# Idle transposes ahead of the first product, and two gate products of the third node tile re-ordered, in a graph network and expert kernel

## The reference

```python
h = layernorm(x)
m = relu(concat(h[src], edge_attr) @ W1.T + b1) @ W2.T + b2
agg = segment_sum(m, dst)
gi, gh = agg @ W_ih.T + b_ih, h @ W_hh.T + b_hh        # three thirds each: r, z, n
r, z = sigmoid(i_r + h_r), sigmoid(i_z + h_z)
n = tanh(i_n + r * h_n)
x1 = x + h + batchnorm((1 - z) * n + z * h)
```

```python
h2 = layernorm(x1)
f1 = h2 @ [Wg | W1 | Ws1]      # 8 gate logits, 256 expert units, 32 shared units
comb = softmax of the two largest gate logits, at their experts
out = x1 + (relu(expert units) * comb) @ W2 + shared part
```

## Time and profile before

| | |
|---|---|
| Median of 3 runs | 1315.35 us (1314.4 to 1319.97) |
| The profiled execution's own time | 1303.76 us |
| Its span, first to last instruction | 1301.9 us |
| Mean granted TensorE clock | 0.999 |
| Busy: TensorE, GpSimd, VectorE, ScalarE | 1281.2, 816.4, 997.7, 734.0 us |

### The profile page before, as it was taken

One profiled execution on the slowest core, in us unless ns is written; L12 is line 12 of the kernel. 1 busy time (PEld: TensorE's weight loads), 2 busy tenths in 40 slices (PEclk: granted clock), 3 DMA queues, 4 the chain that ended last, 5 costly groups with the idle time before them and its releaser, 6 DMA issues. The chain is left out here.

```text
span 1301.9 us, 22928 instructions
## 1 busy us (share of the span) xinstructions
PE 1281.2 (98%) x6398; PEld 1083.2 (83%) x6398; DVE 997.7 (77%) x2198; ACT 734.0 (56%) x1726; POOL 816.4 (63%) x1117
## 2 busy tenths in 40 slices
PE   8999999999899999999999999999999999999997
PEld 7788888888688888888888888888888888888885
DVE  6879575568777777777777777777777777777776
ACT  5331222134666666666666666666666666666652
POOL 3121243114777777777777777777778777777771
PEclk9999999999999999999999999999999999999999
DMA  8123554377433433333433433433433433433430
GB/s 297 43 83 135 198 198 162 125 273 240 141 132 130 135 122 129 137 121 129 137 121 129 136 121 129 136 122 129 137 121 129 137 121 129 137 121 129 136 98 33
DMA packets 64208, 179.58 MB, mean 138 GB/s; under 512 B 9456, under 2 KB 10352, under 8 KB 64048
## 3 DMA queue, kind: packets, MB, share of 16 engines
q1 hardware_dynamic: 48160, 99.20, 22.3%
q0 software_dynamic: 16016, 79.97, 18.6%
HBM read 141.86 MB, written 37.29 MB: 138 GB/s over the span
## 5 line engine op out<-in xcount | busy, mean ns | idle before, releaser
L1844 PE MATMUL bank<-whh_hi,x_hi 128*128 128x512 f32 x948 | 376.7, 397 | 2.4 <-DVE x L1774 1.6
L1844 PE MATMUL bank<-whh_hi,x_lo 128*128 128x512 f32 x948 | 370.1, 390 | 0.0
L1844 PE MATMUL bank<-whh_lo,x_hi 128*128 128x512 f32 x948 | 369.7, 390 | 0.0
L1844 PEld LDWEIGHTS bank<-whh_hi,x_hi 128*128 128x128 f32 x948 | 178.2, 188 | 38.6 <-DVE x L1774 2.0
L1844 PEld LDWEIGHTS bank<-whh_hi,x_lo 128*128 128x128 f32 x948 | 178.0, 188 | 37.8
L1844 PEld LDWEIGHTS bank<-whh_lo,x_hi 128*128 128x128 f32 x948 | 178.3, 188 | 34.3
L1593 POOL TENSOR_TENSOR h_n<-h,n_gate 128x512 f32<-128x512 f32 x78 | 101.0, 1294 | 68.7 <-ACT n_gate L1612 68.7
L1525 POOL TENSOR_TENSOR rstd<-var_eps,minus_half 128x1 f32<-128x1 f32 x158 | 90.4, 572 | 66.0 <-DVE var_eps L505 65.9
L1733 DVE TENSOR_TENSOR h_lo<-bank,h_hi 128x512 fp32r<-128x512 f32 x79 | 54.7, 692 | 77.8 <-ACT h_hi L1660 77.8
L1510 POOL DMA_INDIRECT gates<-gates_in,slot_at x78 | 83.7, 1074 | 46.7 <-issue 45.7
L1587 POOL TENSOR_TENSOR n_pre<-r_hn,gates 128x512 f32<-128x512 f32 x77 | 99.2, 1288 | 13.0 <-POOL r_hn L1583 13.0
(11 more groups left out here) (214 smaller groups left out, 3101.9 us busy)
## 6 DMA issues: line engine op xcount, KB each, us to landing
xt<-in_x SPq DMA_DIRECT2D x79, 256.0 KB, 2.8
x_lo_raw<-in_x_cols SPq DMA_DIRECT2D x79, 256.0 KB, 2.7
out<-y SPq DMA_DIRECT2D x78, 256.0 KB, 2.0
gates_in<-g_out SPq DMA_DIRECT2D x16, 768.0 KB, 3.9
whh_rows<-in_whh SPq DMA_DIRECT2D x4, 768.0 KB, 5.8
whh_lo_raw<-in_whh_t SPq DMA_DIRECT2D x4, 768.0 KB, 10.3
gates_in<-g_out SPq DMA_DIRECT2D x12, 256.0 KB, 4.3
wih_lo_raw<-in_wih_t SPq DMA_DIRECT2D x2, 1024.0 KB, 8.4
```

Of the source, the lines that this page charges most:

```text
L1844: last = pe.matmul(to[0:R, :], a[:, s, k * R:(k + 1) * R], w[:, k, q * D:(q + 1) * D], start=n == 0, stop=n == 3 * DK - 1)
```

## The change

There are three edits. The idle transposes at the start become 17. In period 1 TensorE issues n of tile 2 (`new_gate(pe, p, 1)`) between the turn of h2 of tile 0 and the f1 product of tile 0. In period 2 it issues z of tile 2 whole into bank `b_f2`, behind a wait for z_pre of tile 1, and the second layer of tile 0, which writes the same bank, waits for z_pre of tile 2. All other periods keep their order.

```diff
     def z_bank(p):
-        return b_f2 if p.first(-1) else b_z
+        return b_f2 if p.first(-1) or p.first(-2) else b_z
...
-            keep_running(12)
+            keep_running(17)
...
+            def new_gate(pe, p, k):
+                wait_from(pe, hn_done, p.t + k)
+                gate(p.slot(k), b_n, 2).then_inc(n_prod, 1)
+
             def body(p):
                 t = p.t
+                if p.has(0) and not p.first(-2):
+                    reset_gate(pe, p, 0)
+                    new_gate(pe, p, 0)
                 if p.has(0):
-                    s = p.slot(0)
-                    if not p.first(-2):
-                        reset_gate(pe, p, 0)
-                    wait_from(pe, hn_done, t)
-                    gate(s, b_n, 2).then_inc(n_prod, 1)
-                if p.has(0):
-                    if p.first(-1):
+                    if p.first(-1) or p.first(-2):
+                        if p.first(-2):
+                            pe.wait_ge(z_pre_done, t)
                         gate(p.slot(0), z_bank(p), 1).then_inc(z_prod, 1)
-
-                        reset_gate(pe, p, 1)
                     else:
                         wait_from(pe, x1_done, t)
                         gate(p.slot(0), b_z, 1, 0, 2)
+                if p.first(-1):
+
+                    reset_gate(pe, p, 1)
...
                 if p.last(-1):
                     keep_running(10)
-                if p.has(0) and not p.first(-1):
+                if p.first(-1):
+                    new_gate(pe, p, 1)
+                if p.has(0) and not p.first(-1) and not p.first(-2):
                     gate(p.slot(0), b_z, 1, 2, DK).then_inc(z_prod, 1)
...
                     wait_from(pe, y_done, t - 2)
+                    if p.first(-2):
+                        pe.wait_ge(z_pre_done, t + 1)
                     if p.last(-2):
```

## The result

The changed kernel takes 1318.98 us (median of 10 runs, 1316.3 to 1322.49). The kernel before takes 1315.13 us beside it (median of 10, 1312.76 to 1319.97). The ratio is 1.0027, with a 95% interval of 1.0014 to 1.0040, so it is 1.8 to 5.3 us slower. The forecast was 1316.4 us, in a range from 1312.6 to 1320.2. The order of the cases was wrong. The one that came is rival B, 1318.3 us, to which I gave one chance in five.

What follows compares the result with a forecast made beforehand. TensorE, busy 98% of the span, was taken as the bound. Transposes 0, node-stage pauses removed 1.50 + 1.56 against 3.4 + 1.3 grown or new, gave +1.0 us: from 1315.35 to 1316.4 us, range 1312.6 to 1320.2.

Steps and rivals of the forecast that it cites:

- rival B: Node-stage start-up: the clock falls in the new 4.8 us pause, costing 1.9 us more, together +2.9, 1318.3 us; chance 0.20.
- Pauses are moved, not removed: Node-stage start-up: pauses of 1.50 and 1.56 us go, others grow or appear by 3.4 and 1.3 us.
- f1 is 1.04 us late and takes the chain with it: Node stage: n ahead of the first f1 delays it 1.04 us, moving the second tile's chain from 341.25 to 342.3.
- ending at 341.13: End of VectorE's search for the two best experts, taken as directly ahead of the second tile's chain, which starts at 341.25.
- rival D: Node stage: GpSimd's h_n holds the second tile's chain, hiding f1's delay if also late; parts 2 and 3 give 0; chance 0.10.
- z whole costs its cover: Node stage: without z's second half behind the second h2 turn, a new pause of some 1.3 us precedes the second f1.
- One fall is all the trace has: Argument against the clock falling in the 4.8 us pause: the trace showed only one fall, at the end of the span.
- Transposes: 0, with the time lost at 37 us: Start: first product 1.8 us ahead at best, lost in TensorE's wait for VectorE's searches near 37 us; net 0.
- my lower bound was 0: Start: the five extra transposes were bounded between 0 and -1.8 us, so no loss was allowed for.
- Rival C: Start: timed executions have TensorE late at 37 us, so transposes give back 1.8 us; -0.8 in all, 1314.6 us; chance 0.12.
- +1.0: Sum at the fourth tile's r, starting at 353.8 instead of 352.74, carried to the end of the kernel.

Runs made afterwards that it cites:

- e4: The changed kernel with 38 more idle transposes filling the 4.4 us pause before the second turn of h2; ratio to the kernel before 1.0006.
- e12: The kernel before with z of the third tile whole in its own bank, and 12 idle transposes ahead of the first f1; one run, 1308.13 us.
- e6: The kernel before with only z of the third tile whole and in a bank of its own; ratio 0.9997.
- e3: The changed kernel with 12 idle transposes, so the node-stage edits alone; ratio to the kernel before 1.0022.
- e5: The kernel before with only n of the third tile moved ahead of the first tile's f1; ratio 1.0009.
- e7: The kernel before with 17 idle transposes and two VectorE searches moved from ahead of the first m_lo to behind compare(0); ratio 0.9963.
- e1: The kernel before, unchanged, measured against itself; ratio 1.0011.
- e8: The kernel before with six loads of bias rows moved one group later in SyncE's list; ratio 0.9991.
- e11: As e5, with 36 idle transposes in the pause before z of the third tile; one run, 1308.41 us.
- e2: The kernel before with 17 idle transposes in place of 12, nothing else; ratio 1.0010.
- e9: As e7 with the later bias loads of e8, node stage as in the kernel before; ratio to the kernel before 0.9977.
- e10: As e9, with 12, 13 and 12 idle transposes in three node-stage start-up pauses; ratio to the kernel before 0.9975.

## Why the prediction was right and where it was wrong

- **Pauses are moved, not removed; h2 of the second tile is the chain.** Right. The pause was forecast at 4.8 us and came at 4.43, with 0.77 (1.09 with the clock up, e4) behind it, forecast at 1.3. The number itself landed in the range for a reason to which I gave one chance in five; the point forecast had about a third of the shift.
- **f1 is 1.04 us late and takes the chain with it.** f1 was 1.07 us later against the first turn, 350.87 - 347.64 = 3.23 instead of 2.16. The chain was late by 0.78 only. The step that failed is the one with the tie, "ending at 341.13". I took the search as the releaser of the chain, and it was GpSimd's h_n, as e12's profile names it. In the changed kernel VectorE starts the chain 0.08 us after the search begins (353.74 to 353.82), and before it started it 0.29 us after (340.96 to 341.25), when h_n had ended at 341.15. So rival D was true for 0.2 us. The term is 0.75 us, not 1.0.
- **z whole costs its cover.** Forecast as a new pause before f1. It is there, but it costs nothing of its own: with z alone the second f1 starts on time (e12), and in e6 r follows the second turn by 18.05 - 12.63 = 5.42 us, before by 5.46.
- **The clock.** This is the case that decided, and I put it second. The term was sized well, 1.9 us against 2.0 to 2.4, and its chance badly. The step that failed in the main sum is that it put the clock's fall in the 4.8 us pause at nothing. The long pause brought the fall in all three profiles that had it unfilled (changed kernel, e3, e5). Over the timed runs the loss to the clock grew by 2.3 us. "One fall is all the trace has" was true, and the one fall in the earlier trace rows came 4.2 us after the last work. A forecast pause of 4.8 us was longer than that and should have had the larger chance. In these traces the pauses of 4.43 us (changed kernel, e3) and 4.09 (e5) had a fall, and some of 1.50. The fall that the Trainium skill shows 5.2 us after the last matmul (TensorE: Matmul & The Clock Gate, Seeing it yourself) is no bound: the traces here have falls after less, 4.2 us at the end of the span and 4.43 in the changed kernel.
- **Transposes: 0, with the time lost at 37 us.** Right: the pause grew by the 2.0 us that TensorE was ahead, 0.34 to 2.36, TensorE left at 38.56, and e7 shows what held it. What I missed is the other sign. The longer pause can take the clock down, for 1.6 us (42.98 - 38.56 = 4.4 against 2.8), and my lower bound was 0. Pauses of 1.61 us and more at this place had a fall behind them in five profiles (e1, e4, e8, e11, the changed kernel); those of 1.39 and less, or no pause, had none (before, e2, e3, e5, e6, e12). Eleven profiles of one place are no rule: pauses of 1.50 us did both elsewhere.
- **Rival C** was possible but small. In e3 and e5 the clock rose some 6 us after the first product's start, and TensorE came to 37 us without a pause. It left at 38.95 and 38.55. The nine others with the searches in their old place left between 38.56 and 39.87, so the price of it is inside the scatter of VectorE's own time there. In e1 TensorE was 1.8 us early.
- **The sum.** 0.75 for the chain and 2.0 to 2.4 for the fall, both from profiles, make 2.8 to 3.1 us. The means of the timed runs differ by 3.0, the ratio by 3.6 (1.8 to 5.3). With intervals of this width the agreement is a consistency and no proof. The prediction's list of pauses doesn't add up to its +1.0: 3.4 + 1.3 less 1.50 + 1.56 is 1.6, and the remaining 0.6 isn't rounding. It set idle times as rows print them against gaps between starts. From 336.26 to 338.01 TensorE starts nothing for 1.75 us, where the row says 1.50. The +1.0 stands by the starts alone, 353.8 - 352.74. The prediction also held that nothing under 6.6 us could be told from no change; the interval here leaves out everything under 1.8.

## What to carry to other kernels

Filling a pause of the busiest engine gains nothing where another engine's chain sets the next start, and it loses where the filler is longer than the pause and that chain hangs on the work behind it. Before merging several short pauses into one, ask what the clock does in the long one; here a loss of 0.75 us became 3. A saving ahead of a wait has to be followed to the releaser of that wait: two searches that nobody needed yet held back the gain of the first product, and moving them, with 17 transposes, gave 3 us or more.

## What the hardware showed that I had not expected

- The clock rises and falls at other moments from one execution to the next. After the first product's start it rose at once or within 3 to 6 us later: at once in the changed kernel, e4, e7 and e9, but after 4.6 us in e2 and e10, all with 17 transposes. With 12 it never rose at once, in eight profiles. The same 1.50 us pause kept the clock four times and lost it three times. A single profile of such a pause proves neither.
- The kernel before takes 1315 us on two chips and 1306 on a third, where the profiles of e9 to e12 have no pause near 182 us. The first profile of the kernel before, at 1303.76 us, has none either. On the others ScalarE sometimes starts a_hi, whose operand TensorE has finished, some 5 us late. Why is open.
- From the fourth tile's r to the end any of these kernels takes either 949.2 us (the first profile of the kernel before, e3, e4, e10) or 950.3 to 950.4 (the others), which is 1.1 us of scatter that no edit here touched.
